# Last chunk of a causal attention: row sums of the probabilities taken over pairs of cells added on VectorE

## The chip, the cores and the metric

The kernel runs on one core of a Trainium2 chip. The metric is device time in microseconds (us) of one launch; a kernel is timed in several runs, and one further execution is profiled. The engines are TensorE (PE; its weight loads are listed apart as PEld), VectorE (DVE), ScalarE (ACT), GpSimd (POOL) and SyncE (SP), which issues DMAs.

## What is computed

The program is a small transformer block in fp32 over 2048 rows of width 128: layer norms, two gated linear units with fp4-rounded operands, a linear attention, two ReLU layers, and a causal softmax attention with 16 heads. The change touches the last of these:

```python
Q = _split_heads(x, H)                 # 16 heads of 8
K = _split_heads(x @ Wk + bk, H)
V = _split_heads(x @ Wv + bv, H)       # 16 heads of 32
scores = jnp.einsum('bhqd,bhkd->bhqk', Q, K) + mask
attn = jax.nn.softmax(scores, axis=-1)
o = jnp.einsum('bhqk,bhkd->bhqd', attn, V)
return x + jax.nn.gelu(o, approximate=False) @ Wf + bf
```

Of the softmax three things are done apart: the row maximum (from score products of its own, before the group), the exponentials, and the row sums by which the result is divided in the end.

## The kernel before

The 2048 queries are cut in 4 **chunks** of 512, and the 16 heads in 4 sets of 4, which are two **pairs** of heads. A chunk with one set is a **group**: groups 0 to 15, of which 12 to 15 are the last chunk. A group goes over the keys in **cells** (`CELLS`): a full cell is 128 keys by 512 queries for all four heads. In the last chunk a group has 12 full cells, then the diagonal ones: three joined cells in groups 12 to 14 (keys 0; 2; 1 and 3 of the diagonal), four single ones in group 15. I number the cells of a group from 0.

The order of all work is a list, `PLAN`, built in Python. Each engine takes from it, in order, the steps that it has a part in, and waits on semaphores for the others. `causal` writes the part of the attention: each cell u has two slots.

- Slot u.0: TensorE makes the scores of pair 0 of cell u (L1753, bf16, two matmuls), mostly also one product for a row maximum of the next group (L1718), and then the values product of cell u-1 (L1779, probabilities times V in fp32, four heads side by side in the array's columns).
- Slot u.1: scores of pair 1 of cell u, a maximum, and then the row sums of cell u-1 (L1797): the same probabilities times a matrix of ones, with the same shapes and the same cost as the values.
- Other work of the slot follows behind: the output projection of the finished chunk (L1811) and its last ReLU layer (L1655 transpose, L1665, L1676), GELU, normalisation.

ScalarE takes the exponential of each pair of scores, 128x1024, from PSUM into `pr` in SBUF (L1023), a ring of four cells (`RING`): before it writes cell u it waits for the sums of cell u-4. The values of a cell wait for both of its exponentials. VectorE reduces each product for the maxima, 128x1024 from PSUM (L1370). In the last chunk the maxima of a group are spread over the slots from four cells before the group ahead of it begins to four cells before it begins itself, so group 15 has none beside it, and the last four cells of group 14 neither. Scores and maxima (and some other products) take turns in three **sets** of two PSUM banks: a product waits until what was three turns ago in its set has been read, scores by ScalarE, maxima by VectorE.

At a group's end ScalarE copies the values (L1038) and the sums (L1052) out of PSUM, DMAs gather the sums, VectorE inverts them (`invert`, L1388), DMAs spread them, and GpSimd multiplies (`norm`, L852). In the last group the diagonal tiles are done one by one (L1397, L1400). GELU of a finished chunk runs on ScalarE `GELU_AT` cells behind the chunk's end. In the nine slots ahead of it the scores are issued up to three ahead (`AHEAD`), so that TensorE has probabilities to work with while ScalarE is at the GELU.

## Time and profile before

| what | value |
|---|---|
| median of 3 runs | 1012.1 us (1012.02 to 1012.51) |
| the profiled execution, whole | 1015.57 us |
| its span, from first to last instruction | 1013.8 us |
| mean granted clock of TensorE in it | 0.971 of full speed |
| TensorE, VectorE, ScalarE, GpSimd busy | 88%, 69%, 50%, 26% of the span |
| group 12, between the copies of the group's values | 796.9 to 849.8 us |
| group 13 | 849.8 to 908.4 us |
| group 14 | 908.4 to 953.1 us |
| group 15, up to its diagonal tiles | 953.1 to 987 us |

The three timed runs and the profiled execution are different executions; spans and instruction times are of the profiled one. Busy time of TensorE is modelled, since its matmuls are pipelined, so the time from one weight load to the next is the better measure of what a product costs. In a row of the order of time, the bracket says how long the engine was idle before it, and what released it; "issue" means that it waited for nothing that the profile shows.

### The profile page before, as it was taken

To read this page: it belongs to the slowest core of one execution; us is meant where nothing else is said; L and a number is where in the kernel's file an instruction comes from. 1 tells how busy PE (TensorE), PEld (TensorE's weight loads), DVE (VectorE), ACT (ScalarE), POOL (GpSimd) and SP (SyncE) were. 2 spreads that over 40 slices of the span, in tenths; PEclk is the share of its full clock that TensorE was granted. 3 is DMA by queue.
4 is the path that set the end of the run, shared out by engine and by line. 5 is a ranking of instruction groups with operands and counts; after the bars stand their busy time and mean duration, and the time that the engine had idled before them with its cause. 6 is when DMAs were issued, how large, how long until landed. Compare 5 with 4: busy or idle time off the path is not lost.

```text
span 1013.8 us, 19797 instructions
## 1 busy us (share of the span) xinstructions
PE 888.9 (88%) x7281; PEld 449.0 (44%) x7281; DVE 696.2 (69%) x1678; ACT 508.1 (50%) x867; POOL 260.5 (26%) x409
## 2 busy tenths in 40 slices
PE   2689997777888786888899999999899999999997
PEld 1355536656676665444344434243332224332225
DVE  7899834367888757778775787766588776677104
ACT  1233432233455322453466556755556675666774
POOL 3566410034556755413330000321000000000000
PEclk9999998889999979998999999999999999999999
DMA  8100000000000032140012100001400000000000
GB/s 215 45 1 1 1 0 1 1 1 1 1 2 1 1 66 29 34 67 11 21 46 44 34 18 18 12 3 48 69 12 13 13 2 6 16 4 12 14 1 12
DMA packets 30698, 22.65 MB, mean 22 GB/s; under 512 B 9530, under 2 KB 27786, under 8 KB 30604
## 3 DMA queue, kind: packets, MB, share of 16 engines
q1 hardware_dynamic: 28660, 20.84, 9.5%
q8 instruction: 61, 1.00, 0.4%
q10 hardware_dynamic: 1944, 0.55, 0.3%
q14 instruction: 33, 0.27, 0.1%
HBM read 16.79 MB, written 4.32 MB: 21 GB/s over the span
## 4 chain that ended last, share of the span: by engine, by line
PE 58%; DVE 22%; issue 6%; POOL 5%; ACT 5%; DMA 3%; SPq 1%; ACTq 0%; POOLq 0%; DVEq 0%
PE psum L1779 12%; PE psum L1797 10%; PE psum L1753 7%; PE psum L1718 6%; DVE arena L1370 5%; PE psum L1665 3%; PE psum L1634 2%; POOL rs L745 2%; PE psum L1472 2%; PE psum L1676 2%; ACT arena L1023 2%; PE psum L1563 1%; PE psum L1811 1%; DVE arena L1243 1%; ACT rh L993 1%
## 5 line engine op out<-in xcount | busy, mean ns | idle before, releaser
L1370 DVE TENSOR_REDUCE arena<-psum 128x2 f32<-128x1024 f32 (+2 forms) x320 | 334.4, 1063 | 114.7 <-PE psum L1718 71.7
L1023 ACT ACTIVATE arena<-psum 128x1024 f32<-128x1024 f32 (+3 forms) x298 | 280.5, 950 | 131.0 <-PE psum L1753 75.1
L745 POOL TENSOR_TENSOR rs<-ve,mhalf 128x1 f32<-128x1 f32 x128 | 71.8, 568 | 360.4 <-DVE ve L1152 359.3
L1779 PE MATMUL psum<-arena 128*32 128x512 f32 (+3 forms) x1280 | 148.8, 543 | 0.3 <-ACT arena L1023 0.2
L1797 PE MATMUL psum<-arena,ones 128*32 128x512 f32 (+3 forms) x1280 | 148.0, 541 | 0.9 <-DVE arena L1397 0.8
L1718 PE MATMUL psum<-arena 48*128 48x512 bf16 (+3 forms) x640 | 109.6, 351 | 28.6 <-DVE arena L1370 9.2
L1753 PE MATMUL psum<-arena 50*128 50x512 bf16 (+3 forms) x640 | 111.3, 355 | 5.3 <-DVE X L1351 1.9
L1753 PEld LDWEIGHTS psum<-arena 50*128 50x128 bf16 x640 | 31.0, 93 | 169.9 <-issue 104.1
L852 POOL TENSOR_TENSOR arena<-arena 128x512 f32<-128x512 f32 x15 | 19.1, 1276 | 231.5 <-DMA arena<-scr_sums 231.5
L993 ACT ACTIVATE rh<-psum,fb 128x128 f32<-128x128 f32 x128 | 36.5, 368 | 57.2 <-PE psum L1665 57.1
L1718 PEld LDWEIGHTS psum<-arena 48*128 48x128 bf16 x640 | 35.9, 94 | 62.7 <-DVE arena L1370 21.2
L1472 PE MATMUL psum<-WguT,xqT 128*128 128x352 f32 x128 | 48.6, 506 | 7.5 <-DVE hb L1193 5.4
L1797 PEld LDWEIGHTS psum<-arena,ones 128*32 128x32 f32 x1280 | 26.4, 108 | 33.0 <-issue 28.7
L1779 PEld LDWEIGHTS psum<-arena 128*32 128x32 f32 x1280 | 26.5, 108 | 32.4 <-issue 26.5
L1665 PE MATMUL psum<-xdT,fW 128*128 128x128 f32 x256 | 37.7, 293 | 3.6 <-ACT xdT L983 3.6
L1665 PEld LDWEIGHTS psum<-xdT,fW 128*128 128x128 f32 x256 | 32.8, 200 | 16.9 <-issue 11.5
L749 POOL TENSOR_TENSOR xv<-xv,xm 128x128 f32<-128x128 f32 x32 | 20.2, 630 | 71.4 <-DVE xv L1109 71.4
L931 ACT ACTIVATE arena<-psum,mone 128x1024 f32<-128x1024 f32 x16 | 17.8, 1114 | 40.4 <-PE psum L1510 40.4
L1510 PE MATMUL psum<-arena 128*128 128x512 f32 x64 | 31.3, 611 | 7.2 <-DVE arena L1243 6.9
L1676 PE MATMUL psum<-fW,rh 128*128 128x128 f32 x256 | 36.4, 287 | 0.0
L1472 PEld LDWEIGHTS psum<-WguT,xqT 128*128 128x128 f32 x128 | 25.2, 208 | 24.8 <-issue 13.6
L749 POOL TENSOR_TENSOR hv<-hv,hm 128x352 f32<-128x352 f32 x32 | 29.7, 929 | 23.0 <-DVE hv L1109 23.0
(193 smaller groups left out, 1465.6 us busy)
## 6 DMA issues: line engine op xcount, KB each, us to landing
arena<-scr_parts SPq DMA_DIRECT2D x96, 64.0 KB
arena<-scr_sums SPq DMA_DIRECT2D x60, 64.0 KB, 2.0
scr_parts<-arena SPq DMA_DIRECT2D x12, 256.0 KB, 2.7
arena<-arena SPq DMA_DIRECT2D x124, 2.0 KB, 1.7
X<-in_L_attn_src_dram SPq DMA_DIRECT2D x4, 256.0 KB, 5.1
out_dram<-X SPq DMA_DIRECT2D x16, 64.0 KB, 1.6
arena<-in_L_attn_Wk_dram SPq DMA_DIRECT2D x1, 512.0 KB, 7.1
arena<-in_L_attn_Wq_dram SPq DMA_DIRECT2D x1, 512.0 KB, 8.1
```

The lines of the kernel that those rows point to most:

```text
L745: v.tensor_tensor(rs[:, u, t:t + 1], ve[:, u, t:t + 1], mhalf[:, :], ALU.pow).then_inc(s_rstd[u], 1)
L749: k = me.did(v.tensor_tensor(x, x, m, ALU.subtract))
L993: v.activation(rh[:, n % 2, j, :], bank(bank_d(n, "d_hidden"))[:, P * j:P * j + P], ACT.Relu, bias=fb1[:, j:j + 1]).then_inc(s_relu, 1)
L1023: v.activation(pr[:, u % RING, pp, :, 0:CH - off], both(("scores", n))[0][:, :, off:CH], ACT.Exp).then_inc(s_p, 1)
L1370: v.tensor_reduce(MXP[:, j, 2 * pp:2 * pp + 2, m], both(("max", g, pp, j, m))[0][:, :, 0:hi - lo], AX_X, ALU.max).then_inc(s_mxd, 1)
L1472: last = mm(bank(b + k)[:, 0:GI], xqT[:, n % 2, :], WguT[:, k, :], start=True, stop=True)
L1665: last = mm(bank(b)[:, P * j:P * j + P], fW1[:, P * j:P * j + P], xdT[:, n % 2, :], start=True, stop=True)
L1676: last = mm(bank(b)[:, P:2 * P], rh[:, n % 2, j, :], fW2[:, j, :], start=False, stop=(j == FJ - 1), skip_group_check=True)
L1718: last = mm(o[:, par, 0:w], QS[c % 2][r, hp, P * j:P * j + P], KK[m][r, hp, 0:w], start=True, stop=(m < c), skip_group_check=True)
L1753: last = mm(o[:, par, at:at + CH - off], KK[kb // TPC][r, hp, P * (kb % TPC):P * (kb % TPC) + P], QS[c % 2][r, hp, off:CH], start=True, st ...
L1779: last = mm(bank(O_BANK)[VD * h:VD * h + VD, off:CH], V[kb // TPC][:, kb % TPC, GH * (g % GPC) + h, :], pr[:, u % RING, h // 2, h % 2, at: ...
L1797: last = mm(bank(D_BANK)[VD * h:VD * h + VD, off:CH], ones1[:, 0:VD], pr[:, u % RING, h // 2, h % 2, at:at + CH - off], start=(kb == 0), s ...
```

## The change

Four full cells in a row, u to u+3, become a **quad** in the last chunk, where none of them lies in the stretch with scores issued ahead: cells 0 to 3 and 4 to 7 in group 12, and also 8 to 11 in groups 13, 14 and 15, eleven quads in all. For each quad VectorE makes two additions in place in the ring, each of 128x1024 in fp32 (`presum`): for pair 0 it adds the probabilities of cell u+1 to those of cell u, in slot u+1.1; for pair 1 those of cell u+2 to those of cell u+1, in slot u+3.0. Each waits for the exponential that it reads and for the values product of the cell that it writes. Then three sets of row sums serve the four cells: (pair 0 of u with u+1, pair 1 of u), (pair 0 of u+2, pair 1 of u+1 with u+2), and (cell u+3). They stand in the slots u+3.1, u+4.1 and u+5.1; in the last quad of a group the third goes to u+4.1 as well. The first two wait for the additions (`s_pre`). The ring is freed by the set that a cell ends in (`FREED`).

Two tables of numbers change too: the GELU of chunk 2, with the projection and the ReLU layer behind it, moves from 9 to 13 cells behind the chunk's end, which is into group 12 or 13; GpSimd's normalisation moves from 5 to 8 cells behind a group's end in chunk 2, and from 7 to 12 in the last chunk.

```diff
--- before.py
+++ after.py
@@ -76,10 +76,11 @@
 MAX_LEAD = 4
 
 INVERT_AT = {0: 3, 1: 5, 2: 3, 3: 2}
-NORM_AT = {0: 5, 1: 6, 2: 5, 3: 7}
-GELU_AT = {0: 10, 1: 8, 2: 9, 3: 1}
+NORM_AT = {0: 5, 1: 6, 2: 8, 3: 12}
+GELU_AT = {0: 10, 1: 8, 2: 13, 3: 1}
 JOINED = [(0,), (2,), (1, 3)]
 JOINED_FROM = 4
+PRESUM_FROM = 12
 RELU_BEHIND = 4
 RELU_TILE = 3
 AHEAD = ((9, 6, 1), (6, 3, 2), (3, 0, 3))
@@ -351,6 +352,7 @@
         s_att = sem("keys_set")
         s_mx, s_mxd, s_mxn, s_mt, s_mp = sem("mx"), sem("mx_reduced"), sem("mx_row"), sem("mx_turned"), sem("mx_parts")
         s_mq = [sem("mx_loaded_0"), sem("mx_loaded_1")]
+        s_pre = sem("probs_added")
         s_st, s_p, s_av, s_dn = sem("scores"), sem("probs"), sem("av"), sem("dn")
         s_ot, s_dt, s_rd, s_on, s_onl, s_og = (sem("o_copied"), sem("dn_copied"), sem("dn_inverted"), sem("o_normed"),
                                                sem("last_o_normed"), sem("o_gelu"))
@@ -384,6 +386,34 @@
 
         CELLS = [(g, x) for g in range(MGROUPS) for x in cells_of(g)]
         GROUP_U = [CELLS.index((g, cells_of(g)[0])) for g in range(MGROUPS)] + [len(CELLS)]
+
+        PRESUMS, SUMS, SUMS_AT, PRESUMS_AT, FREED, SUMS_END = [], [], {}, {}, {}, []
+
+        def add_sums(at, first, second, adds, frees):
+
+            SUMS_AT.setdefault(at, []).append(len(SUMS))
+            SUMS.append((first, second, adds))
+            FREED.update({u: len(SUMS) for u in frees})
+
+        for g in range(MGROUPS):
+            u, end = GROUP_U[g], GROUP_U[g + 1]
+            while u < end:
+                ahead_there = g % GPC == 0 and CELLS[u][1][0] >= TPC * (g // GPC - 1)
+                if g >= PRESUM_FROM and not ahead_there and CELLS[u][1][0] + TPC <= TPC * (g // GPC):
+                    PRESUMS_AT.setdefault((u + 1, 1), []).append(len(PRESUMS))
+                    PRESUMS.append((0, u, u + 1))
+                    PRESUMS_AT.setdefault((u + 3, 0), []).append(len(PRESUMS))
+                    PRESUMS.append((1, u + 1, u + 2))
+                    n = len(PRESUMS)
+                    add_sums(u + 3, u, u, n - 1, (u,))
+                    add_sums(u + 4, u + 2, u + 1, n, (u + 1, u + 2))
+                    last_quad = CELLS[u + 4][1][0] >= TPC * (g // GPC - (g % GPC == 0))
+                    add_sums(u + 4 if last_quad else u + 5, u + 3, u + 3, n, (u + 3,))
+                    u += 4
+                else:
+                    add_sums(u + 1, u, u, len(PRESUMS), (u,))
+                    u += 1
+            SUMS_END.append(len(SUMS))
 
         def strips(u):
 
@@ -534,12 +564,16 @@
                         scored += 1
                     out += [x for x in slot if x[0] == "max"]
                     if 0 < u <= len(CELLS):
-                        out.append(("values" if i == 0 else "sums", u - 1))
+                        if i == 0:
+                            out.append(("values", u - 1))
+                        else:
+                            out += [("sums", d) for d in SUMS_AT.get(u, [])]
                         g, x = CELLS[u - 1]
                         if g == LAST and x[0] >= TPC * (CHUNKS - 1):
                             out.append(("take_tile" if i == 0 else "invert_tile", x[0] % TPC))
                         elif u == GROUP_U[g + 1]:
                             out.append(("take_o" if i == 0 else "take_d", g))
+                    out += [("presum", k) for k in PRESUMS_AT.get((u, i), [])]
                     out += others[cut * i:cut * (i + 1)] + [x for x in slot if x[0] not in ("row_max", "max")]
 
             ready, held = [], []
@@ -1019,7 +1053,7 @@
                     act.wait_ge(s_xb, GROUPS)
                     act.wait_ge(s_y, GROUPS)
                 if u >= RING:
-                    act.wait_ge(s_dn, u - RING + 1)
+                    act.wait_ge(s_dn, FREED[u - RING])
                 v.activation(pr[:, u % RING, pp, :, 0:CH - off], both(("scores", n))[0][:, :, off:CH], ACT.Exp
                              ).then_inc(s_p, 1)
 
@@ -1046,7 +1080,7 @@
                 v.copy(GT[LAST // GPC % 2][:, LAST % GPC, q], bank(O_BANK)[:, q]).then_inc(s_otl, 1)
 
             def take_d(g):
-                act.wait_ge(s_dn, GROUP_U[g + 1])
+                act.wait_ge(s_dn, SUMS_END[g])
                 if g >= 2:
                     act.wait_ge(s_on, g - 1)
                 v.copy(DN[g % 2], bank(D_BANK)).then_inc(s_dt, 1)
@@ -1383,6 +1417,15 @@
                 me.wait(k)
                 v.tensor_tensor(MXS[:, :, :, 1], MXS[:, :, :, 0], MXH, ALU.subtract).then_inc(s_mxn, 1)
 
+            def presum(k):
+
+                pp, u, v_u = PRESUMS[k]
+                dve.wait_ge(s_p, GP * v_u + pp + 1)
+                dve.wait_ge(s_av, u + 1)
+                p = pr[:, u % RING, pp, :, :].rearrange("p h q -> p (h q)")
+                v.tensor_tensor(p, p, pr[:, v_u % RING, pp, :, :].rearrange("p h q -> p (h q)"), ALU.add
+                                ).then_inc(s_pre, 1)
+
             def invert(g):
                 dve.wait_ge(s_dg[g % 2], 16 * GH * (g // 2 + 1))
                 v.reciprocal(DG[g % 2], DG[g % 2]).then_inc(s_rd, 1)
@@ -1391,7 +1434,7 @@
 
                 q = slice(P * j, P * j + P)
                 r, o = DN[LAST % 2][:, q], GT[LAST // GPC % 2][:, LAST % GPC, q]
-                dve.wait_ge(s_dn, GROUP_U[LAST] + TPC * (CHUNKS - 1) + j + 1)
+                dve.wait_ge(s_dn, SUMS_END[LAST] - TPC + j + 1)
                 if j == 0:
                     dve.wait_ge(s_on, LAST - 1)
                 v.reciprocal(r, bank(D_BANK)[:, q]).then_inc(s_dtl, 1)
@@ -1410,7 +1453,7 @@
                    q_scale), out_add=out_add, out_norm=out_norm, y_add=y_add, y_norm=y_norm,
                    add_stats_d=add_stats_d, f_stats=f_stats, d_norm=d_norm, d_add=d_add, e_stats=e_stats,
                    e_norm=e_norm, max=take_max, row_max=row_max,
-                   invert=invert, invert_tile=invert_tile, wf=add_wf)
+                   invert=invert, presum=presum, invert_tile=invert_tile, wf=add_wf)
 
         @block.tensor
         def _(pe):
@@ -1784,19 +1827,22 @@
                 if end:
                     B[O_BANK].read_by((s_ot, g + 1))
 
-            def sums(u):
-                g, x = CELLS[u]
+            def sums(d):
+                *cells, adds = SUMS[d]
+                g, x = CELLS[cells[0]]
                 c = g // GPC
-                end = u + 1 == GROUP_U[g + 1]
+                end = d + 1 == SUMS_END[g]
                 if x[0] == 0:
                     B[D_BANK].free(pe)
                 if g == LAST and x[0] > TPC * (CHUNKS - 1):
                     pe.wait_ge(s_dtl, x[0] - TPC * (CHUNKS - 1))
-                for kb, off, _, at in strips(u)[0]:
+                if d and adds > SUMS[d - 1][2]:
+                    pe.wait_ge(s_pre, adds)
+                for k, (kb, off, _, at) in enumerate(strips(cells[0])[0]):
                     for h in range(GH):
                         last = mm(bank(D_BANK)[VD * h:VD * h + VD, off:CH], ones1[:, 0:VD],
-                                  pr[:, u % RING, h // 2, h % 2, at:at + CH - off], start=(kb == 0), stop=end,
-                                  skip_group_check=True)
+                                  pr[:, cells[h // 2] % RING, h // 2, h % 2, at:at + CH - off], start=(kb == 0),
+                                  stop=end, skip_group_check=True)
                 last.then_inc(s_dn, 1)
                 if end:
                     B[D_BANK].read_by((s_dt, g + 1))
```

TensorE at the start of group 14, from the scores of slot 1.1 to those of slot 3.1. Before (L1753 scores, L1718 maxima, L1724 their mask, L1779 values, L1797 row sums):

```order
L1753 MATMUL psum<-arena 128x512 x2
L1718 MATMUL psum<-arena 128x512 x2
L1797 MATMUL psum<-arena,ones 32x512 x4
L1753 MATMUL psum<-arena 128x512 x2
L1718 MATMUL psum<-arena 128x512 x2
L1779 MATMUL psum<-arena 32x512 x4
L1753 MATMUL psum<-arena 128x512 x2
L1718 MATMUL psum<-arena 128x512 x2
L1797 MATMUL psum<-arena,ones 32x512 x4
L1753 MATMUL psum<-arena 128x512 x2
L1718 MATMUL psum<-arena 128x512 x2
L1724 MATMUL psum<-ident,mask_kq 128x64 x4
```

And now, at the same place (the same steps are L1796, L1761, L1767, L1822 and L1843):

```order
L1796 MATMUL psum<-arena 128x512 x2
L1761 MATMUL psum<-arena 128x512 x2
L1796 MATMUL psum<-arena 128x512 x2
L1761 MATMUL psum<-arena 128x512 x2
L1822 MATMUL psum<-arena 32x512 x4
L1796 MATMUL psum<-arena 128x512 x2
L1761 MATMUL psum<-arena 128x512 x2
L1796 MATMUL psum<-arena 128x512 x2
L1761 MATMUL psum<-arena 128x512 x2
L1767 MATMUL psum<-ident,mask_kq 128x64 x4
```

The row sums of the slots 1.1 and 2.1 are gone, and scores and maximum of one slot stand directly behind those of the slot before. The sums of slot 3.1 are the first of the quad.

VectorE over most of group 14, from its first addition on (L1404 reduces a maximum, L1426 adds, L1431 inverts the sums of group 13):

```order
L1426 TENSOR_TENSOR arena<-arena 128x1024
L1404 TENSOR_REDUCE arena<-psum 128x2
L1431 RECIPROCAL arena<-arena 128x16
L1404 TENSOR_REDUCE arena<-psum 128x2 x2
L1426 TENSOR_TENSOR arena<-arena 128x1024
L1404 TENSOR_REDUCE arena<-psum 128x2 x6
L1426 TENSOR_TENSOR arena<-arena 128x1024
L1404 TENSOR_REDUCE arena<-psum 128x2 x3
L1426 TENSOR_TENSOR arena<-arena 128x1024
L1404 TENSOR_REDUCE arena<-psum 128x2 x5
```

Before, VectorE had only the reductions and the reciprocal there. Five additions stand between them now, each ahead of reductions whose products hold a PSUM set.

TensorE at the end of group 14, from the values of cell 11 on, now:

```order
L1822 MATMUL psum<-arena 32x512 x4
L1796 MATMUL psum<-arena 128x512 x2
L1803 MATMUL psum<-ident,mask_qk 128x64 x4
L1843 MATMUL psum<-arena,ones 32x512 x8
L1796 MATMUL psum<-arena 128x256 x2
```

The row sums of slot 12.1 are two sets, eight matmuls in place of four.

## Rows read from the trace of the kernel before

**Rows 1.** The page: span; busy time, share and instructions of engines.

```profile
span 1013.8 us, 19797 instructions
...
PE 888.9 (88%) x7281; PEld 449.0 (44%) x7281; DVE 696.2 (69%) x1678; ACT 508.1 (50%) x867; POOL 260.5 (26%) x409
```

**Rows 2.** Stretches: us; busy PE, PEld, DVE, ACT, POOL; PEclk; DMA share; GB/s.

```profile
796.90:849.80 52.90, 51.90 (x489) 17.00 (x481) 38.02 (x44) 35.47 (x40) 1.83 (x2) 1.00 0.03 7
849.80:908.40 58.60, 57.03 (x529) 21.20 (x531) 39.95 (x53) 35.88 (x55) 2.89 (x4) 1.00 0.04 11
908.40:953.10 44.70, 44.47 (x430) 12.16 (x430) 25.55 (x26) 31.20 (x35) 1.28 (x1) 1.00 0.03 8
953.10:987.00 33.90, 33.82 (x280) 7.02 (x274) 0.25 (x1) 26.70 (x28) 1.28 (x1) 1.00 0.03 9
...
908.40:938.00 29.60, 29.60 (x262) 7.61 (x262) 22.72 (x22) 20.30 (x22) 1.28 (x1) 1.00 0.04 11
```

**Rows 3.** Order of time, group 15: start, duration, engine, operation [idle, releaser].

```profile
957.83 0.10 PEld L1753 LDWEIGHTS psum<-arena 50*128 50x128 bf16 x2 [0.84 <-issue]
...
958.26 1.02 ACT L1023 ACTIVATE arena<-psum 128x1024 f32<-128x1024 f32 x1 [0.29 <-PE psum L1753]
...
959.14 0.10 PEld L1753 LDWEIGHTS psum<-arena 50*128 50x128 bf16 x2 [0.84 <-issue]
...
959.47 0.16 PEld L1779 LDWEIGHTS psum<-arena 128*32 128x32 f32 x8 [0.23 <-ACT arena L1023]
```

**Rows 4.** Order of time, group 14, slots with one maximum each.

```profile
910.85 0.10 PEld L1753 LDWEIGHTS psum<-arena 50*128 50x128 bf16 x2 [0.84 <-issue]
...
911.39 0.16 PEld L1797 LDWEIGHTS psum<-arena,ones 128*32 128x32 f32 x8 [0.23 <-issue]
...
912.39 0.10 PEld L1753 LDWEIGHTS psum<-arena 50*128 50x128 bf16 x2 [0.84 <-issue]
...
912.93 0.16 PEld L1779 LDWEIGHTS psum<-arena 128*32 128x32 f32 x8 [0.38 <-issue]
...
913.04 1.23 DVE L1370 TENSOR_REDUCE arena<-psum 128x2 f32<-128x1024 f32 x1 [0.31 <-PE psum L1718]
```

**Rows 5.** Order of time, end of group 13: exponential, maximum, values.

```profile
905.24 1.02 ACT L1023 ACTIVATE arena<-psum 128x1024 f32<-128x1024 f32 x1 [0.17 <-PE psum L1760]
...
906.38 0.12 PEld L1718 LDWEIGHTS psum<-arena 48*128 48x128 bf16 x2 [0.17 <-ACT arena L1023]
...
906.73 0.16 PEld L1779 LDWEIGHTS psum<-arena 128*32 128x32 f32 x8 [0.23 <-issue]
```

**Rows 6.** Groups of VectorE instructions, shapes apart: count, busy us, mean ns.

```profile
L1370 DVE TENSOR_REDUCE arena<-psum 128x2 f32<-128x1024 f32 x224 | 271.4, 1224 | 83.7 <-PE psum L1718 71.7 <-PE psum L1724 10.1
...
L1370 DVE TENSOR_REDUCE arena<-psum 128x2 f32<-128x256 f32 x32 | 13.5, 421 | 8.5 <-PE psum L1724 8.5
...
L1109 DVE TENSOR_TENSOR hv<-hv,hm 128x352 f32<-128x352 f32 x32 | 16.6, 520 | 0.2
...
L1120 DVE TENSOR_TENSOR arena<-arena 128x768 f32<-128x768 f32 x1 | 1.0, 958 | 0.0
```

**Rows 7.** Order of time, group 14, first quad, with two maxima at 917.

```profile
909.27 0.10 PEld L1753 LDWEIGHTS psum<-arena 50*128 50x128 bf16 x2 [0.20 <-issue]
...
917.51 0.13 PEld L1718 LDWEIGHTS psum<-arena 48*128 48x128 bf16 x2 [0.34 <-DVE arena L1370]
...
917.71 3.82 DVE L1370 TENSOR_REDUCE arena<-psum 128x2 f32<-128x1024 f32 x4 [0.31 <-PE psum L1718]
...
919.05 0.12 PEld L1718 LDWEIGHTS psum<-arena 48*128 48x128 bf16 x2
...
921.83 0.10 PEld L1753 LDWEIGHTS psum<-arena 50*128 50x128 bf16 x2 [0.84 <-DVE arena L1370]
```

**Rows 8.** Order of time, group 12, scores issued ahead of the GELU.

```profile
809.72 0.12 PEld L1718 LDWEIGHTS psum<-arena 48*128 48x128 bf16 x2 [0.75 <-DVE arena L1370]
...
816.66 0.13 PEld L1718 LDWEIGHTS psum<-arena 48*128 48x128 bf16 x2 [0.59 <-ACT arena L1023]
```

## The prediction

> **What bounds the kernel now.** I read the page's first part, then the table of stretches for the last four groups, then the instructions in order of time for a few microseconds of each kind of cell. Groups are numbered 12 to 15 in the last chunk, cells from 0 in each group; slot c.0 is scores of pair 0, a row maximum, values of cell c-1; slot c.1 is scores of pair 1, a maximum, row sums. TensorE is busy 88% of the span [rows 1] and nearly all of each of these four stretches, at full granted clock, while VectorE is at 72%, 68%, 57% and then idle [rows 2]. Read naively, every row sum taken off TensorE is time gained. The order of time says something narrower. Without maxima (group 15) a slot takes 1.31 us (957.83 to 959.14), and the values of cell c start when the second exponential of cell c is just done: it starts 0.43 us after its scores, lasts 1.02, ends at 959.28, and the values' weights load at 959.47, with ScalarE named as releaser [rows 3]. From scores c.1 to values c is 1.64 us. So row sums lie exactly where TensorE would otherwise wait for the exponential. With maxima a slot takes 1.54 us and the same distance is 2.08 (910.85 to 912.93) [rows 4]; the slack is small there too, because scores and maxima share three PSUM sets and the maximum of slot c+1.0 takes the set that the scores of slot c.1 filled. It must wait for that exponential: 905.24 + 1.02 = 906.26, next maximum at 906.38, values at 906.73 [rows 5]. I take from this: exponential end plus 0.12 to the maximum, plus 0.35 to the values.
>
> **What the change removes.** Eleven quads (two in group 12, three each in 13 to 15) have three sets of row sums instead of four. A set costs TensorE 0.99 to 1.00 us, from its weight load to the next scores [rows 4]: 911.39 to 912.39. Were all eleven on the path, 10.9 us would go.
>
> **Where the sets go.** They are not spread evenly. The slots 1.1, 2.1, 6.1 and (groups 13 to 15) 10.1 have no sums now, which is 3 + 4 + 4 + 4 = 15 empty slots, and the last quad of each group puts two sets into one slot (8.1 in group 12, 12.1 in the others), which is 4 doubled slots; 15 - 4 = 11. The two kinds have to be priced apart.
>
> A **doubled slot** costs a full set: it stands in a stretch where TensorE waits for nothing, and nobody gives the microsecond back. 4 x 0.99 = **+4.0 us**. Bounds 0 (if it covers a wait of its own) and 4.0; I take 4.0, since the rows around it show no wait.
>
> An **empty slot without maxima** leaves scores c.1, scores c+1.0, values c: the distance is 0.43 + 1.02 + 0.12 = 1.57 to 0.19 for the last term = 1.64, against 1.64 before [rows 3]. Gain 0 to 0.07 each, four in group 15: **-0.1 us**.
>
> An **empty slot with maxima** goes to 0.43 + 1.02 + 0.12 + 0.35 = 1.92 against 2.08 [rows 4, 5]: 0.16 us, not 0.99. Three in second quads and two in third quads (the one of group 14 has no maximum behind it and may give 0.36, that of group 13 has a transpose in it and gives about 0): together **-0.9 us**. The six in first quads stand in the next term.
>
> **The additions on VectorE.** 22 of them, 128x1024 in fp32. The trace has none of that size; 128x768 took 0.958 us and 128x352 0.520, so (0.958 - 0.520)/416 = 1.05 ns an element and 1.23 us for 1024 [rows 6], the same as a maximum of 1024 (1.224). Back to back the pitch is shorter: four maxima in 3.82 us, one of them of 0.42, give (3.82 - 0.42)/3 = 1.13 us [rows 6, 7]. In group 15 VectorE is free, and each addition is issued two slots or more before the sums that wait for it: no cost. Its wait for the values of the cell before and for the exponentials is met at once, as both stand earlier in TensorE's order. The Trainium skill, "VectorE: DVE Perf Modes", section "Mode 1x (REGULAR) - the baseline", gives such a two-tensor fp32 operation one result per cycle, and its Specifications 0.96 GHz; an estimate from that page would be 1.07 us, and the additions would cost a few tenths of a microsecond less in all. The rows of this trace, with their fixed part, say more, and they are what I use.
>
> With maxima VectorE is nearly full locally: from 908.4 to 938.0, the part of group 14 with maxima, it is busy 22.7 of 29.6 us [rows 2]; five additions at 1.13 bring that to 28.4. And TensorE is issued against it with three PSUM sets of slack. I walk the first quad of group 14, where slot 3.1 has two maxima, from scores 1.0 (909.27) as zero. Scores 1.1 at 1.58, its maximum starts to be reduced 0.65 later (as 912.39 to 913.04 in [rows 4]), from 2.2 to 3.4, and the first addition follows to 4.5. Scores 2.0 at 2.12, values 1 at 3.50 (before 3.66). The maximum of 2.0 is reduced 4.5 to 5.7, after it comes a small reciprocal (0.2 allowed), that of 2.1 from 5.84 to 7.06, which delays scores 3.0 to 5.83; that wait is hidden, as the maximum behind it has to wait for the exponential until 6.07 anyway. Maximum 3.0 is reduced 6.97 to 8.19, then the second addition to 9.23. Scores 3.1 at 7.58; its second maximum needs the set that is free at 8.19 + 0.12. Its first maximum is reduced only 9.23 to 10.45. Scores 4.0 at 9.65, but the maximum of 4.0 needs that set: 10.57 in place of 9.78. In the run before the same reduction ended at 918.93 and the maximum was issued at 919.05, just in time [rows 7]; so there is no slack to eat. Values 3 are 0.79 late, scores 5.0 at 13.33 against 12.56: **+0.8 us** with two empty slots in it; with a pitch of 1.22 in place of 1.13 the same walk gives +1.2. I take 1.0. Group 12 has the same rows in its first quad: 1.0 again. In group 13 the products of the output projection stand between and give VectorE time; the same walk gives +0.4. Together **+2.4 us**. Bounds: -1.0 (six times 0.16, additions free) and +3.5.
>
> **The moved steps.** GELU of chunk 2 goes from cell 9 to cell 13 of group 12, with its three scores ahead. Those cost TensorE waits now: 0.75 us for VectorE in slot 4.1 and 0.59 for ScalarE in 6.1 [rows 8]; with others like them I put it at some 1.8 us over the slots 4.1 to 8.1. At the new place the first of these slots has the doubled sums, which cover a wait, and the diagonal cells have shorter exponentials; behind it the same work comes. I take **-0.6**, bounds -1.8 and +0.8. GpSimd's normalisation moves from 5 to 8 and 7 to 12 cells behind the group's end; GpSimd is busy 1.3 to 2.9 us per group [rows 2], nothing waits for it before the GELU of its chunk: 0. The last one has no other GpSimd work ahead of it in group 15.
>
> **Sum.** 4.0 - 0.1 - 0.9 + 2.4 - 0.6 = **+4.8 us**. The profiled execution had a span of 1013.8 and took 1015.57 in all; the median of three is 1012.1. The difference stands between spans; I add it to the median: **1016.9 us**.
>
> **The rivals.**
> (a) *Every removed set counts.* For it: TensorE at 88 to 99%, VectorE with 15 to 19 us free in groups 12 to 14 and all of group 15. Against it: [rows 3, 5], where values wait for the exponential. It gives 1012.1 - 10.9 = 1001.2. The Trainium skill speaks for this one: "Perfetto Trace Analysis", section "Identifying the Most-Contended Engine", says to find the engine with the highest occupancy and to optimise that one first, and by that the 10.9 us would come off; the trace disagrees, as [rows 3] show TensorE tied to ScalarE. The same section warns that matmul busy time is no good measure of how close TensorE is to its limit, and with that the trace agrees. Chance 0.06.
> (b) *The empty slots fill by half.* Score products ahead, transposes and the hidden layer of chunk 2 lie in the waits, so that an empty slot gives 0.55 us: 15 x 0.55 = 8.3, less 4.0 for the doubled ones and 0.6 for the move: 1007.2. Against it: the other work is nearly always placed behind the values, in c.0, not in the empty slot. Chance 0.12.
> (c) *The doubled slots are free*, since scores and maxima behind them find their sets ready and recover what was lost: +4.8 - 4.0 = +0.8: 1012.9. Chance 0.14.
> (d) *VectorE becomes the bound*: each of the seven pairs of additions in groups 12 to 14 costs what the worked pair costs (0.8 to 1.2 and its lost relief of 0.3, so 1.3), 7.5 x 1.3 = 9.8 in place of 2.4: 1024.3. This decides where the backlog is not gone when the next pair comes. Against it: in the walk it is gone by slot 5.1. Chance 0.08.
> My forecast, slower by the doubled slots and two or three late maxima, has 0.60, with its own range of 1014.1 to 1020.0.
>
> **How the numbers follow.** A measurement of this kernel tells 0.2% (2.0 us) from no change. Faster: (a) and (b), 0.18. Same: most of (c), 0.12. Slower: the forecast, (d) and a rest of (c), 0.70. The range reaches from (b) to the top of the forecast, 1007.0 to 1020.0, and leaves out (a), (d) and little more.
>
> **What would show it.** In the profile after: in group 15, scores c.1 to values c in an empty slot should still be 1.57 to 1.64 us, with ScalarE as releaser of the values (at 0.65 the forecast is wrong and (a) right). In groups 12 to 14, 1.9 us in empty slots with maxima. In the slots 8.1 and 12.1 two sets should take 2.0 us and scores follow at once; if the slots behind are shorter than before, (c). In the first quads of groups 12 and 14 the maximum of slot 4.0 should wait 0.7 us or more for VectorE; if it doesn't, that term falls away and the sum is +3.0 or less. An addition should take 1.23 us. If group 15 is shorter than before from its first cell to its last full one, the forecast is wrong at its root.

## The result: slower, by more than forecast

| | kernel before | changed kernel |
|---|---|---|
| runs beside each other | 1015.43 us median of 7 (1012.02 to 1017.1) | 1023.06 us median of 7 (1019.27 to 1027.4) |
| ratio | | 1.0084, 95% interval 1.0056 to 1.0112 |
| profiled execution, span | 1013.8 us | 1017.5 us |

The direction was forecast, 1016.9 us, and the size was not: 1023.06 us lies above the range (1007.0 to 1020.0). Two things add up. The first three runs of the kernel before had a median of 1012.1; 31 runs of it beside the first experiments had 1016.5 (1009.51 to 1023.59), so part of the distance is the base. The rest is in the kernel.

The page of the changed kernel, the lines that answer [rows 1]:

```profile
span 1017.5 us, 19657 instructions
...
PE 875.3 (86%) x7181; PEld 445.9 (44%) x7193; DVE 719.4 (71%) x1700; ACT 507.8 (50%) x867; POOL 260.5 (26%) x409
...
L1426 DVE TENSOR_TENSOR arena<-arena 128x1024 f32<-128x1024 f32 x22 | 26.8, 1218 | 30.3 <-ACT arena L1057 30.3
```

TensorE has 13.6 us less to do and VectorE 23.2 us more, of which 26.8 are the 22 additions, and the span is longer. The stretches of groups 12 to 15, as in [rows 2] (us; busy PE, PEld, DVE, ACT, POOL; granted clock; DMA share; GB/s):

```profile
794.90:846.20 51.30, 47.03 (x448) 14.29 (x443) 40.27 (x41) 35.65 (x40) 1.28 (x1) 1.00 0.02 7
846.20:910.30 64.10, 57.21 (x520) 22.90 (x520) 48.00 (x64) 35.95 (x53) 3.42 (x5) 1.00 0.04 9
910.30:957.50 47.20, 43.20 (x414) 12.34 (x417) 31.64 (x33) 31.16 (x34) 1.28 (x1) 1.00 0.04 9
957.50:991.70 34.20, 30.51 (x256) 6.28 (x250) 7.60 (x7) 26.26 (x28) 1.27 (x1) 1.00 0.04 10
```

TensorE stood still for 1.0, 1.6, 0.2 and 0.1 us in these stretches before, and for 4.3, 6.9, 4.0 and 3.7 us now, at full granted clock both times.

**The measure used below.** Single runs of one kernel lie up to 14 us apart, but the time from one copy of a group's values (`take_o`) to the next repeats within 0.03 us between executions of kernels with the same code there. Group 15 is counted from its last such copy to the load of ScalarE's table for the last GELU. All that differs between executions lies outside groups 12 to 15. "Before" in the experiments means these lengths of the profiled execution of the kernel before:

| run | group 12 | 13 | 14 | 15 | sum |
|---|---|---|---|---|---|
| kernel before | 52.94 | 58.65 | 44.67 | 40.27 | 196.53 |
| changed kernel | 51.25 | 64.09 | 47.23 | 40.61 | 203.18 |
| x1_moves | 49.67 | 61.42 | 45.77 | 40.27 | 197.13 |
| x2_empty_slots | 49.92 | 61.01 | 45.09 | 39.74 | 195.76 |
| x3_no_additions | 49.92 | 61.87 | 45.95 | 40.61 | 198.35 |
| x4_changed_again | 51.25 | 64.08 | 47.24 | 40.61 | 203.18 |
| x9_first_quads | 50.93 | 62.83 | 46.98 | 40.60 | 201.34 |
| x8_norm_only | 52.93 | 58.66 | 44.67 | 40.26 | 196.52 |
| x5_group15 | 52.94 | 58.67 | 44.67 | 40.61 | 196.89 |
| x6_group15_ahead | 52.93 | 58.66 | 45.18 | 36.36 | 193.13 |
| x7_ahead_only | 52.94 | 58.66 | 45.19 | 39.14 | 195.93 |
| x10_pairs | 52.93 | 58.65 | 45.18 | 38.63 | 195.39 |
| x11_later_inverse | 52.94 | 58.65 | 45.18 | 36.36 | 193.13 |
| x12_ahead_again | 52.94 | 58.65 | 45.18 | 36.36 | 193.13 |

The changed kernel loses 6.65 us in these groups: -1.69, +5.44, +2.56 and +0.34.

### The profile page after: what moved, and what is told of

The parts are those of the page before. It is cut to its first block, busy times and chain, and to the rows that moved or that the text cites. A ratio compares the mean times of both kernels' runs of the same rounds, so it can differ in the third digit from the quotient of the medians.

```text
span 1017.5 us, 19657 instructions
## 1 busy us (share of the span) xinstructions
PE 875.3 (86%) x7181; PEld 445.9 (44%) x7193; DVE 719.4 (71%) x1700; ACT 507.8 (50%) x867; POOL 260.5 (26%) x409
## 4 chain that ended last, share of the span: by engine, by line
PE 52%; DVE 27%; issue 7%; ACT 5%; POOL 5%; DMA 3%; SPq 0%; ACTq 0%; DVEq 0%; POOLq 0%
PE psum L1822 10%; PE psum L1843 8%; DVE arena L1404 8%; PE psum L1796 5%; PE psum L1761 5%; PE psum L1708 3%; PE psum L1677 2%; ACT arena L1057 2%; POOL rs L779 2%; PE psum L1515 2%; PE psum L1719 2%; PE psum L1606 1%; DVE arena L1426 1%; ACT rh L1027 1%; DVE arena L1277 1%
## 5 line engine op out<-in xcount | busy, mean ns | idle before, releaser
L1404 DVE TENSOR_REDUCE arena<-psum 128x2 f32<-128x1024 f32 (+2 forms) x320 | 333.0, 1061 | 106.9 <-PE psum L1761 67.4
L1057 ACT ACTIVATE arena<-psum 128x1024 f32<-128x1024 f32 (+3 forms) x298 | 279.9, 950 | 136.2 <-PE psum L1796 79.1
L1822 PE MATMUL psum<-arena 128*32 128x512 f32 (+3 forms) x1280 | 148.3, 541 | 3.9 <-ACT arena L1057 3.8
L1761 PE MATMUL psum<-arena 48*128 48x512 bf16 (+3 forms) x640 | 109.5, 349 | 35.4 <-DVE arena L1404 13.0
L1843 PE MATMUL psum<-arena,ones 128*32 128x512 f32 (+3 forms) x1192 | 135.2, 535 | 0.9 <-DVE arena L1440 0.8
L1796 PE MATMUL psum<-arena 50*128 50x512 bf16 (+3 forms) x640 | 110.4, 353 | 9.0 <-DVE arena L1404 4.7
L1796 PEld LDWEIGHTS psum<-arena 50*128 50x128 bf16 x640 | 30.9, 92 | 164.3 <-issue 87.7
L1761 PEld LDWEIGHTS psum<-arena 48*128 48x128 bf16 x640 | 35.8, 93 | 71.8 <-DVE arena L1404 26.8
L1426 DVE TENSOR_TENSOR arena<-arena 128x1024 f32<-128x1024 f32 x22 | 26.8, 1218 | 30.3 <-ACT arena L1057 30.3
L1822 PEld LDWEIGHTS psum<-arena 128*32 128x32 f32 x1280 | 26.4, 108 | 36.8 <-issue 25.7
L1843 PEld LDWEIGHTS psum<-arena,ones 128*32 128x32 f32 x1192 | 25.0, 108 | 32.7 <-issue 28.2
L1515 PEld LDWEIGHTS psum<-WguT,xqT 128*128 128x128 f32 x128 | 25.1, 207 | 24.8 <-issue 13.6
```

Of the source, the lines that this page charges most:

```text
L1057: v.activation(pr[:, u % RING, pp, :, 0:CH - off], both(("scores", n))[0][:, :, off:CH], ACT.Exp).then_inc(s_p, 1)
L1404: v.tensor_reduce(MXP[:, j, 2 * pp:2 * pp + 2, m], both(("max", g, pp, j, m))[0][:, :, 0:hi - lo], AX_X, ALU.max).then_inc(s_mxd, 1)
L1426: v.tensor_tensor(p, p, pr[:, v_u % RING, pp, :, :].rearrange("p h q -> p (h q)"), ALU.add).then_inc(s_pre, 1)
L1515: last = mm(bank(b + k)[:, 0:GI], xqT[:, n % 2, :], WguT[:, k, :], start=True, stop=True)
L1761: last = mm(o[:, par, 0:w], QS[c % 2][r, hp, P * j:P * j + P], KK[m][r, hp, 0:w], start=True, stop=(m < c), skip_group_check=True)
L1796: last = mm(o[:, par, at:at + CH - off], KK[kb // TPC][r, hp, P * (kb % TPC):P * (kb % TPC) + P], QS[c % 2][r, hp, off:CH], start=True, st ...
```

## What the rows of the changed kernel show

**Empty slot without maxima**, group 15 (order of time: start, duration, engine, operation, idle before and releaser; scores are L1796, values L1822, exponentials L1057):

```profile
959.58 0.12 PEld L1796 LDWEIGHTS psum<-arena 50*128 50x128 bf16 x4 [0.84 <-issue]
960.01 1.94 ACT L1057 ACTIVATE arena<-psum 128x1024 f32<-128x1024 f32 x2 [0.17 <-PE psum L1796]
961.09 0.16 PEld L1822 LDWEIGHTS psum<-arena 128*32 128x32 f32 x8 [1.40 <-ACT arena L1057]
961.09 1.06 PE L1822 MATMUL psum<-arena 128*32 128x512 f32 x8 [0.90 <-ACT arena L1057]
```

The row "x4" holds the scores of both slots, since no sums stand between them. From them to the values it is 1.51 us, with the exponential as releaser, where [rows 3] had 1.64 with a set of row sums inside. So a removed set gives 0.13 us. No weights are loaded for 1.40 us, and TensorE itself, which has the four score products to finish first, stands still for 0.90 us. That is nearly the whole set that was taken off it.

**Empty slot with maxima**, group 14 (maxima are L1761):

```profile
913.75 0.10 PEld L1796 LDWEIGHTS psum<-arena 50*128 50x128 bf16 x2 [0.84 <-issue]
913.97 0.12 PEld L1761 LDWEIGHTS psum<-arena 48*128 48x128 bf16 x2
914.09 0.13 PEld L1796 LDWEIGHTS psum<-arena 50*128 50x128 bf16 x2
915.32 0.12 PEld L1761 LDWEIGHTS psum<-arena 48*128 48x128 bf16 x2 [1.10 <-ACT arena L1057]
915.67 0.16 PEld L1822 LDWEIGHTS psum<-arena 128*32 128x32 f32 x8 [0.23 <-issue]
```

From 913.75 to 915.67 it is 1.92 us, the forecast to the hundredth, and by the mechanism it named: the maximum waits for the PSUM set that the exponential reads, and the values stand behind it.

**Doubled slot**, group 15 (sums are L1843):

```profile
988.11 0.10 PEld L1796 LDWEIGHTS psum<-arena 50*128 50x128 bf16 x2 [0.84 <-issue]
...
988.49 0.16 PEld L1843 LDWEIGHTS psum<-arena,ones 128*32 128x32 f32 x8
988.95 0.13 PEld L1843 LDWEIGHTS psum<-arena,ones 128*32 128x32 f32 x4 [0.30 <-issue]
989.38 0.13 PEld L1843 LDWEIGHTS psum<-arena,ones 128*32 128x32 f32 x4 [0.30 <-issue]
990.35 0.10 PEld L1796 LDWEIGHTS psum<-arena 50*128 50x128 bf16 x2 [0.84 <-ACT arena L1057]
```

Two sets (16 loads in all) take 1.86 us, so 0.86 beyond one.

**A late maximum**, first quad of group 14, weight loads and then VectorE (additions are L1426, reductions L1404):

```profile
921.75 0.10 PEld L1796 LDWEIGHTS psum<-arena 50*128 50x128 bf16 x2 [0.84 <-ACT arena L1057]
922.67 0.13 PEld L1761 LDWEIGHTS psum<-arena 48*128 48x128 bf16 x2 [0.82 <-DVE arena L1404]
...
925.45 0.10 PEld L1796 LDWEIGHTS psum<-arena 50*128 50x128 bf16 x2 [0.84 <-DVE arena L1404]
```

```profile
915.57 1.22 DVE L1426 TENSOR_TENSOR arena<-arena 128x1024 f32<-128x1024 f32 x1
...
920.20 1.22 DVE L1426 TENSOR_TENSOR arena<-arena 128x1024 f32<-128x1024 f32 x1
921.33 3.81 DVE L1404 TENSOR_REDUCE arena<-psum 128x2 f32<-128x1024 f32 x4
```

The walk put the maximum of slot 4.0 0.79 us late and scores 5.0 at 13.33 us; the rows have 0.82 us of waiting for VectorE, with four reductions queued behind the addition, and 925.45 - 912.20 = 13.25.

## The experiments

Each edit is against the changed kernel unless it says otherwise. The kernels without additions (x2, x3, and x9 behind the first quad of a group) leave those out, so that the sums lack one head pair of a cell where a pair would be read; x2 also leaves out the last set of each group's last quad. The times of these kernels are of use, their output is not.

**1. x1_moves: only the two tables, no quads.**

```
-PRESUM_FROM = 12
+PRESUM_FROM = 16
```

> The changed kernel with no quads at all: all four sets of row sums per four cells as before, and only the two tables of numbers moved (GELU of chunk 2 to cell 13 of group 12, the normalisation 3 and 5 cells later). It is the control for the next three. My theory (slots tied to the exponential, price of the change from the doubled slots and the additions): 0.6 us below the kernel before, within 1.8 below and 0.8 above. Rival (the moves are what costs time, since the projection and the hidden layer now fall into groups 13 and 14): 3 to 8 us above the kernel before.

Measured: 1015.71 us, ratio 0.9989 (0.9958 to 1.002). Groups 12 to 15 take +0.60 us against before: -3.27, +2.77, +1.10, 0.00. Three products of the output projection (L1857 in these kernels) cross from group 12 into 13 and one of the ReLU layer from 13 into 14. Each takes 1.11 us from its first weight load to the next scores, which makes -3.33, +2.22 and +1.11; what is left is +0.06, +0.55 and -0.01. So the stretch with scores ahead costs group 12 as much at its new place as at the old one, and nearly all of the 0.60 us stands in group 13, among the products that came into it. The waits that should vanish stand at the new place in x1:

```profile
822.54 0.13 PEld L1761 LDWEIGHTS psum<-arena 48*128 48x128 bf16 x2 [0.58 <-ACT arena L1057]
...
827.91 0.12 PEld L1761 LDWEIGHTS psum<-arena 48*128 48x128 bf16 x2 [0.59 <-ACT arena L1057]
...
832.71 0.12 PEld L1796 LDWEIGHTS psum<-arena 50*128 50x128 bf16 x2 [0.72 <-DVE arena L1404]
```

0.75 and 0.59 us were read at the old place [rows 8]; the scores ahead brought their waits with them.

**2. x2_empty_slots: the removed sets, with neither doubled slots nor additions.**

```
-                    PRESUMS_AT.setdefault((u + 1, 1), []).append(len(PRESUMS))
-                    PRESUMS.append((0, u, u + 1))
...
-                    add_sums(u + 4 if last_quad else u + 5, u + 3, u + 3, n, (u + 3,))
+                    if last_quad:
+                        FREED[u + 3] = len(SUMS)
+                    else:
+                        add_sums(u + 5, u + 3, u + 3, n, (u + 3,))
```

> The same as the control, and the row sums of the slots 1.1, 2.1, 6.1 and 10.1 are gone, 15 sets in all, with no additions on VectorE and no doubled slots. It leaves out these parts of the row sums, so its output is divided by too small sums. My theory: an empty slot gives 0.16 us with maxima and 0.07 to 0.13 without, so 2.0 to 2.5 us below the control. In an empty slot the values wait for ScalarE, or the maximum ahead of them does. Rival (a), every set counts: 14.9 us below the control. Rival (b), half of it: 8.3 us below.

Measured: 1017.37 us, ratio 1.0006 (0.9972 to 1.004). Against x1: +0.25, -0.41, -0.68, -0.53, together -1.37 us for fifteen sets less. Fifteen sets are 15 us of TensorE's work, and a tenth of it shows. This is the case for the mechanism of the forecast: the row sums stood where TensorE waits anyway. In group 15 it is 0.13 us for each of four.

That group 12 is longer, not shorter, has a cause of its own. Up to the row sums of slot 8.1 it is 0.41 us ahead of x1 (25.07 us in place of 25.48), for its three empty slots; behind them it is 0.66 us later (24.85 in place of 24.19). These sums load at 822.33:

```profile
823.52 1.94 ACT L1056 ACTIVATE arena<-psum 128x1024 f32<-128x1024 f32 x2 [0.55 <-PE psum L1842]
...
824.66 0.12 PEld L1760 LDWEIGHTS psum<-arena 48*128 48x128 bf16 x2 [1.24 <-ACT arena L1056]
```

The exponential of cell 9 has its scores early, as they are issued ahead here, and waits for the row sums (L1842): in a quad, the sums of cell 5 come in slot 8.1 in place of 6.1, and only they free its place in the ring of four cells. The next maximum waits 1.24 us where x1 has 0.58. The same wait is in the changed kernel, and the forecast has no term for it. Without it, the empty slots give 2.03 us.

**3. x3_no_additions: the sets as in the changed kernel, without VectorE's additions.** (The first four lines of the edit above, and the doubled slots left in.)

> The changed kernel without the additions on VectorE and without the waits for them; row sums in the same slots as in the changed kernel, so 15 empty and 4 doubled slots. It leaves out the additions, so its row sums miss a part. My theory: 4.0 us above the kernel with the empty slots alone, 0.87 to 0.99 in each doubled slot. Rival (c), the doubled slots are free: no difference to it, under 1 us.

Measured: 1017.45 us, ratio 0.9989 (0.9961 to 1.0016). Against x2: 0.00, +0.86, +0.86, +0.87. A doubled slot costs 0.86 us in groups 13 to 15, the same as the rows above, and nothing in group 12. There the first set of slot 8.1 is what the exponential of cell 9 waits for, as in x2; the second set runs while ScalarE works, and from the first set to the end of the group it is 24.85 us in both.

**4. x4_changed_again: the changed kernel once more, on the chip of 1 to 3.**

> The changed kernel once more, for a profile on the same chip as the three others. My theory: 3.4 us above the kernel without additions (1.3 in the first quads of groups 12 and 14, 0.7 in that of group 13 and little elsewhere), and 4 to 6 us above the kernel before. Rival (d), VectorE is the bound in groups 12 to 14: 8 us or more above the kernel without additions.

Measured: 1022.87 us, ratio 1.0066 (1.0036 to 1.0095), the same lengths as in its first profile to 0.01 us. Against x3: +1.33, +2.21, +1.29, 0.00: the additions cost 4.83 us and are the largest term. The same place of group 14 without them (x3; scores L1792, maxima L1757):

```profile
923.01 0.10 PEld L1792 LDWEIGHTS psum<-arena 50*128 50x128 bf16 x2 [0.84 <-ACT arena L1053]
923.21 0.12 PEld L1757 LDWEIGHTS psum<-arena 48*128 48x128 bf16 x2
```

The maximum follows its scores after 0.20 us, with the additions after 0.92.

**5. x9_first_quads: additions in the first quad of each group alone.**

```
+                    first = u == GROUP_U[g]
+                    if first:
...
-                    add_sums(u + 3, u, u, n - 1, (u,))
+                    add_sums(u + 3, u, u, n - 1 if first else n, (u,))
```

> The changed kernel with VectorE's additions in the first quad of each group alone; the other quads keep the places of their sums and their three sets, but the pairs of cells are not added there (those row sums miss a cell of one head pair). What the forecast held: the additions cost only in first quads, so groups 12 to 14 take the 51.25, 64.08 and 47.24 us of the changed kernel. Theory after the runs before: in group 13 the additions of the second and third quads cost 1.2 of their 2.21 us, so group 13 takes 62.8 to 63.0 us (61.87 without any addition), while group 12 stays at 51.2 and group 14 at 47.2.

Measured: 1021.15 us (one run). Against x3 the first quads cost 1.01, 0.96 and 1.03 us; the other quads' additions, changed kernel less x9, 0.32, 1.26 and 0.25. So the walk of the first quad was right in kind, and what the forecast took as free behind it is not, least of all in group 13. There the product of the maximum in slot 8.0 waits in the changed kernel:

```profile
876.34 0.10 PEld L1796 LDWEIGHTS psum<-arena 50*128 50x128 bf16 x2
877.26 0.12 PEld L1761 LDWEIGHTS psum<-arena 48*128 48x128 bf16 x2 [0.83 <-DVE arena L1404]
```

```profile
872.84 0.34 DVE L1191 TENSOR_SCALAR xd<-X,mv,rs 128x128 f32<-128x128 f32 x1
873.65 1.23 DVE L1404 TENSOR_REDUCE arena<-psum 128x2 f32<-128x1024 f32 x1 [0.48 <-PE psum L1761]
874.79 1.22 DVE L1426 TENSOR_TENSOR arena<-arena 128x1024 f32<-128x1024 f32 x1
875.93 1.22 DVE L1404 TENSOR_REDUCE arena<-psum 128x2 f32<-128x1024 f32 x1
```

In x9, without these additions, the same maximum follows its scores (879.74) after 0.20 us in place of 0.92:

```profile
879.94 0.12 PEld L1763 LDWEIGHTS psum<-arena 48*128 48x128 bf16 x2
```

VectorE is without a gap from 873.65 to 877.15 in the changed kernel, and in group 13 it has the ReLU layer's small steps (L1180 to L1191) beside the reductions.

**6. x8_norm_only: the kernel before with the normalisation at its new places.**

```
-GELU_AT = {0: 10, 1: 8, 2: 13, 3: 1}
-PRESUM_FROM = 12
+GELU_AT = {0: 10, 1: 8, 2: 9, 3: 1}
+PRESUM_FROM = 16
```

> The kernel before with GpSimd's normalisation alone at its new places, no quads, GELU of chunk 2 where it was. Theory (all of +0.60 us of the moved steps comes from the products that move with the GELU): groups 12 to 15 take 52.94, 58.65, 44.67 and 40.27 us as before. Rival: the later normalisation holds back the GELU of its chunk or take_o, and group 12 or 15 is longer by some tenths.

Measured: 1015.33 us (one run); all four lengths as before within 0.01. The normalisation costs nothing in them (group 9, in chunk 2, takes 49.56 us in place of 49.45), and the 0.60 us of x1 is the GELU's and that of the work behind it.

**7. x5_group15: quads in group 15 alone, both tables as before.** (`PRESUM_FROM = 15`.)

> Three-set quads in group 15 alone, everything else as in the kernel before (no maxima there, VectorE free). Forecast's theory: four empty slots give 0 to 0.13 us each, the doubled slot 12.1 costs 0.86 to 0.99: group 15 takes 40.61 us in place of 40.27, as it did in the changed kernel, and groups 12 to 14 take 52.94, 58.65 and 44.67 us as before. Rival (interaction: group 15 of the changed kernel was long because of what groups 12 to 14 left behind): group 15 is shorter than 40.27 here.

Measured: 1020.35 us (one run); group 15 takes 40.61 us, +0.34: 0.87 for the doubled slot less four times 0.13. It does not depend on the groups ahead of it.

**8. x6_group15_ahead: the same, with the scores of group 15's full cells one slot further ahead of the values.**

```
+            ahead.update({k: 1 for k in range(2 * GROUP_U[LAST], 2 * GROUP_U[LAST] + 2 * TPC * (CHUNKS - 1))})
```

> As the run before, and the score products of group 15's full cells are issued one slot further ahead of the values, so that the exponential has one more slot to end in. Theory (in the empty slots TensorE waits only for the exponential of the scores just ahead): with that wait gone the three removed sets count, about 0.9 us each, and the doubled slot costs nothing net: group 15 takes 36.8 to 38.5 us in place of 40.61 (ScalarE then has 24 exponentials of 1.02 us in the 12 full cells, 24.5 us, and does not bind), about 3 us less in the span than the kernel with quads in group 15 and no lead. Rival 1 (ScalarE or the PSUM sets bind behind it): group 15 stays above 39.5. Rival 2 (the lead alone gives the gain): the same appears in the control without quads.

Measured: 1014.65 us median of 12 beside 1016.56 for the kernel before (23 runs), ratio 0.9977 (0.9956 to 0.9998). Group 15 takes 36.36 us, 4.25 less than x5, and group 14 0.51 more, since the first scores ahead are issued in it: 3.76 less in all. It went a little below the 36.8 of the theory. An empty slot now (scores L1797, values L1823):

```profile
969.11 0.11 PEld L1797 LDWEIGHTS psum<-arena 50*128 50x128 bf16 x4 [0.84 <-ACT arena L1058]
969.64 0.16 PEld L1823 LDWEIGHTS psum<-arena 128*32 128x32 f32 x8 [0.42 <-ACT arena L1058]
```

From the scores to the values it is 0.53 us where it was 1.51.

**9. x7_ahead_only: the control, the lead without quads.** (`PRESUM_FROM = 16` in the kernel of 8.)

> Control: four sets of row sums per quad as in the kernel before, and only the lead of one slot in group 15's full cells. Theory: TensorE already had its row sums in the place of the wait, of which 0.0 to 0.13 us per slot was left, so group 15 takes 39.0 to 40.3 us in place of 40.27. Rival (the lead alone gives the gain): 38 us or less.

Measured: 1017.24 us, ratio 0.9993 (0.9967 to 1.0018); group 15 39.14 us, 1.13 less than before, 0.60 less in all with group 14. So the two edits are worth +0.36 (quads alone), -0.60 (lead alone) and -3.40 us (both). With the lead, three sets removed give 2.80 us, 0.93 each; without it they give a loss. It settles what the removed sets are worth: nearly their whole cost, once the exponential is no longer what the values wait for.

**10. x10_pairs: with the lead, both head pairs of each second cell added, six sets of twelve removed.** (`PRESUM_FROM = 15` and both tables as in 8.)

```
...
+                    for v in (u, u + 2):
+                        for pp in (0, 1):
+                            PRESUMS_AT.setdefault((v + 1 + pp, 1 - pp), []).append(len(PRESUMS))
+                            PRESUMS.append((pp, v, v + 1))
+                        add_sums(v + 2, v, v, len(PRESUMS), (v, v + 1))
```

> In group 15 alone, with the lead of one slot: both head pairs of each second full cell are added (12 additions of 1.22 us by the idle VectorE), so six of twelve sets of row sums go. Theory: every set removed counts while ScalarE does not bind (24 exponentials of 1.02 us are 24.5 us for the 12 full cells, against 12 x 2.63 - 6 x 0.93 = 26.0 us of TensorE), so group 15 takes 39.14 - 6 x 0.93 = 33.6 us, 2.8 less than with three sets removed, and the whole is 0.5 to 0.8% faster than the kernel before. Rival (the ring of four cells or an addition not ready in time holds the exponential or the sums back): 35 us or more.

Measured: 1012.35 us median of 12 beside 1014.83 (17 runs), ratio 0.9977 (0.9952 to 1.0002); group 15 38.63 us, where the theory said 33.6. The rival holds: the sums wait for the additions (sums L1840, additions L1423).

```profile
965.23 0.10 PEld L1793 LDWEIGHTS psum<-arena 50*128 50x128 bf16 x2 [0.84 <-ACT arena L1054]
967.38 0.16 PEld L1840 LDWEIGHTS psum<-arena,ones 128*32 128x32 f32 x8 [2.05 <-DVE arena L1423]
```

```profile
963.91 3.42 DVE L1423 TENSOR_TENSOR arena<-arena 128x1024 f32<-128x1024 f32 x2 [2.58 <-ACT arena L1054]
```

The four other such waits for an addition are of 0.9 to 1.0 us. The additions of one cell stand in a row behind its second exponential, 2.36 us, and the sums come one slot too early for that. TensorE itself stands still for additions six times, 5.0 us in all, which is the whole distance from 33.6 to 38.63. The 3.42 us of this row are two additions of which the first alone took 2.28, while GpSimd multiplied beside it:

```profile
963.91 2.28 DVE L1423 TENSOR_TENSOR arena<-arena 128x1024 f32<-128x1024 f32 x1 [2.58 <-ACT arena L1054]
963.83 1.28 POOL L883 TENSOR_TENSOR arena<-arena 128x512 f32<-128x512 f32 x1 [44.52 <-DMA arena<-scr_sums]
```

The last section has more on this. There is no run with a later slot for the sums, or with a fifth cell in the ring.

**11. x11_later_inverse: experiment 8 with the inverse of the row sums two cells later in chunk 2.**

```
-INVERT_AT = {0: 3, 1: 5, 2: 3, 3: 2}
-NORM_AT = {0: 5, 1: 6, 2: 5, 3: 7}
+INVERT_AT = {0: 3, 1: 5, 2: 5, 3: 2}
+NORM_AT = {0: 5, 1: 6, 2: 8, 3: 7}
```

(Against experiment 8. The normalisation of chunk 2 is three cells later with it.)

> Three-set quads in group 15 with the lead of one slot, and in chunk 2 VectorE's reciprocal of a group's row sums five cells behind the group's end in place of three (its normalisation eight in place of five). In ten profiled runs so far VectorE waits 0.9 to 5.8 us in group 10 for the transfer that brings the row sums of group 9, while the key blocks of chunk 3 are loaded, and group 10 takes 42.1 to 47.6 us along with it, with the same instructions. Theory (that wait is what makes group 10 vary): two cells later the transfer has landed, VectorE's wait is gone and group 10 takes 41 to 42.3 us, 1 to 5 us less than without this edit, groups 12 to 15 unchanged at 52.9, 58.7, 45.2 and 36.4; the whole is 0.4 to 0.6% faster than the kernel before. Rival (the wait only moves to the later place, or something else varies there): group 10 stays in 42 to 47 us.

**12. x12_ahead_again: experiment 8 once more, on the same chip as 11.**

> The kernel with quads in group 15 and the lead of one slot once more, unchanged, on the same chip as the run with the later reciprocal. Theory: groups 12 to 15 take 52.93, 58.66, 45.18 and 36.36 us again to 0.05 us, and group 10 differs from the 43.42 us of its first run as far as VectorE's wait for the transfer differs from 3.12 us; the run with the later reciprocal is 1 to 3 us faster in the median. Rival: no difference between the two medians.

Measured: x11 1013.02 us, ratio 0.9986 (0.9965 to 1.0006), x12 1012.42 us, ratio 0.997 (0.9948 to 0.9993), both medians of 12 beside 1014.58 for the kernel before (23 runs). In x12 groups 12 to 15 repeat to 0.02 us, and group 10 follows the wait, 43.31 us with 3.01. In x11 VectorE's wait is gone (last section), but group 10 takes 44.56 us and group 11 38.28 in place of 37.18: the gain of the theory didn't come, and group 10 lies where the rival had it. The edit had a second effect, which the last section shows: in both groups GpSimd's multiplication now falls beside a small step of VectorE and holds it up. So x11 doesn't measure what the removed wait is worth by itself. Of the two, x12 is the kernel to keep; its two comparisons lie at 0.3 to 0.2% below the kernel before, and the lengths give 3.4 us, 0.34%.

## Why the prediction was right in direction and short in size

| step | forecast | measured | by |
|---|---|---|---|
| moved steps | -0.6 | +0.60 | x1, x8 |
| empty slots, first quads' included | -2.0 | -1.37 | x2 less x1 |
| doubled slots | +4.0 | +2.59 | x3 less x2 |
| additions alone | +3.4 | +4.83 | x4 less x3 |
| sum | +4.8 | +6.65 | |

The forecast had its -1.0 for the six empty slots of the first quads inside the +2.4 of the additions; here they stand with the other empty slots.

- **What bounds the kernel** was right, and it is the point on which the direction hung. Rival (a), by which every removed set counts and the kernel comes out at 1001.2, is out by x2: 1.37 us for 15 sets. Rival (b), half of each, would have been -8.3. The Trainium skill, "Perfetto Trace Analysis", section "Identifying the Most-Contended Engine", would have one optimise the engine with the highest occupancy first, and warns that the busy share of matmuls doesn't tell how near TensorE is to its limit. The runs bear out the warning: TensorE was busy 33.82 of 33.90 us in group 15 [rows 2], and taking work off it there gave a loss in x5; in x6 the same edit gave 2.8 us, after the wait for another engine was gone.
- **Empty slots**: the sizes worked out slot by slot held (1.92 us with maxima; 1.51 without, within 0.06 of the forecast's 1.57), and so does their sum: 2.03 us without the wait of slot 8.1 in group 12. That wait, 0.66 us for the ring that a quad frees later, is a term that the forecast put at nothing without a reason.
- **Doubled slots**: the term is over-sized. 0.86, not 0.99, and only three of four. The fourth, 8.1 in group 12, hides behind the wait for the ring. That the doubled sums there cover a wait was written down under the moved steps and left out here. With the 0.66 us of that wait, the ends of the quads cost 3.25 us in place of 4.0. Rival (c), free doubled slots, is true of that one alone.
- **Additions**: this is the term that was most under-sized. The first quads cost 1.01, 0.96 and 1.03 (forecast 1.3, 0.7, 1.3 before the relief of empty slots). The step that failed is the rule that an addition behind the first quad costs nothing: 1.83 us, of which 1.26 in group 13. I had looked at free time in a whole stretch (68% busy) and walked only the quads with two maxima in one slot. Rival (d), each pair costing 1.3 us, has the right mechanism for group 13 and too high a price: 9.8 us by its own count of seven and a half pairs (groups 12 to 14 have eight quads), against 4.83.
- **Moved steps**: the sign is wrong, inside the bounds of -1.8 and +0.8. I counted the waits at the old place as removed and put too little at the new one, where they stand as before (+0.06 us in group 12), and gave nothing to what the later projection does to group 13 (+0.55).
- **The range** left out (d) and took the base from three runs. With +6.65 on the 1015.43 of the same comparison it is 1022.1, and 1023.06 was measured; on 1012.1 it would have been 1018.8, inside the range. So of the 6.2 us between the forecast of 1016.9 and the measured 1023.06, 3.3 are the base, 1.85 the terms above (+1.43 additions, +1.20 moved steps, +0.63 empty slots with the ring, -1.41 doubled slots), and 1.0 shows in no length of these groups. The span of the profile moved by 3.7 us alone, as that execution of the changed kernel was 1.0 us quicker in group 10, 1.0 in the last part and 0.9 elsewhere ahead of group 12, of which the change touches at most the normalisation of chunk 2 (group 9 was 0.10 us longer).

## What to carry to other kernels

An engine that is busy all the time can still be paced by another: look at which wait ends last at the instruction behind the one you remove, and price the removal as the distance to that wait. Remove the wait first (here one more score product in flight), then the work; either alone was worth at most 0.6 us, both 3.4. Work handed to an engine that is 70% busy has to be walked through each place where it lands, not only the first, because the queue behind it is what others wait for. And a step that is put off also frees its buffer later: where other work runs ahead, that can become the wait (0.66 us here).
